# LSTM cross-attention step: first exponential's sum on VectorE, first alpha copy on ScalarE, and three reorderings

## What is computed

```python
def attend(h):
    q = h @ Wq.T
    scores = jnp.einsum('bc,bsc->bs', q, context)
    alpha = jax.nn.softmax(scores, axis=-1)
    ctx = jnp.einsum('bs,bsc->bc', alpha, context)
    return jnp.tanh(jnp.concatenate([ctx, h], axis=-1) @ Wout.T + b_out)

def step(carry, x_t):
    h, c, attn = carry
    inp = jnp.concatenate([x_t, attn], axis=-1)
    gates = inp @ W_ih.T + b_ih + h @ W_hh.T + b_hh
    i, f, g, o = jnp.split(gates, 4, axis=-1)
    c = jax.nn.sigmoid(f) * c + jax.nn.sigmoid(i) * jnp.tanh(g)
    h = jax.nn.sigmoid(o) * jnp.tanh(c)
    out = attn_out = attend(h)
    return ((h, c, attn_out), out)
```

## Time and profile before

| | us |
|---|---|
| median of 3 runs (lowest, highest) | 5821.21 (5819.37, 5823.24) |
| the profiled execution, its own time | 5820.65 |
| its span, first to last instruction | 5818.9 |
| busy: TensorE products | 5284.4 (91%) |
| busy: VectorE | 3434.9 (59%) |
| busy: ScalarE | 1981.9 (34%) |
| busy: GpSimd | 347.5 (6%) |

### The profile page before, as it was taken

One profiled execution on the slowest core, in us unless ns is written; L12 is line 12 of the kernel. 1 busy time (PEld: TensorE's weight loads), 2 busy tenths in 40 slices (PEclk: granted clock), 3 DMA queues, 4 the chain that ended last, 5 costly groups with the idle time before them and its releaser, 6 DMA issues. The chain is left out here.

```text
span 5818.9 us, 383675 instructions
## 1 busy us (share of the span) xinstructions
PE 5284.4 (91%) x171240; PEld 3831.9 (66%) x171240; DVE 3434.9 (59%) x15922; ACT 1981.9 (34%) x7977; POOL 347.5 (6%) x795
## 2 busy tenths in 40 slices
PE   9899999999999999999999999998788879797989
PEld 4677777777777777777777777776534334443433
DVE  5455555555555555555555555554698999999931
ACT  2233343434333343434343434333222222223221
POOL 0000000000000000000000000000111111112100
PEclk9999999999999999999999999999888889898989
DMA  2000000000000000000000000002211101010111
GB/s 98 35 2 2 2 2 2 2 2 2 2 2 2 2 2 2 2 2 2 2 2 2 2 2 2 2 2 59 70 44 42 41 18 54 27 51 29 53 37 54
DMA packets 45677, 111.60 MB, mean 19 GB/s; under 512 B 8192, under 2 KB 10240, under 8 KB 45072
## 3 DMA queue, kind: packets, MB, share of 16 engines
q1 hardware_dynamic: 44144, 109.39, 6.0%
q10 hardware_dynamic: 1440, 1.06, 0.1%
HBM read 99.90 MB, written 10.52 MB: 19 GB/s over the span
## 5 line engine op out<-in xcount | busy, mean ns | idle before, releaser
L850 PE MATMUL lstm_part_ps<-lstm_keys,lstm_hid 128*4 128x128 f32 x32768 | 1023.8, 273 | 205.8 <-DVE lstm_hid L1019 205.8
L850 PEld LDWEIGHTS lstm_part_ps<-lstm_keys,lstm_hid 128*4 128x4 f32 x32768 | 770.0, 86 | 428.9 <-DVE lstm_hid L1019 415.2
L866 PE MATMUL lstm_ctx_ps<-lstm_values,lstm_alpha 128*4 128x128 f32 (+1 forms) x49152 | 1050.9, 237 | 0.0
L866 PEld LDWEIGHTS lstm_ctx_ps<-lstm_values,lstm_alpha 128*4 128x4 f32 x49152 | 903.1, 86 | 91.1
L1048 DVE TENSOR_REDUCE lstm_neg_max<-lstm_part_ps 128x1 f32<-128x128 f32 x1024 | 299.0, 292 | 677.7 <-PE lstm_part_ps L850 677.7
L982 ACT ACTIVATE lstm_expo<-lstm_part_ps,lstm_neg_max 128x128 f32<-128x128 f32 x1024 | 377.1, 368 | 861.1 <-DVE lstm_neg_max L1048 861.1
L1001 DVE STREAM_TRANSPOSE lstm_gates<-lstm_half_ps 128x96 f32<-128x96 f32 x1026 | 290.0, 283 | 599.7 <-PE lstm_half_ps L809 575.7
L809 PE MATMUL lstm_half_ps<-lstm_w_hid,lstm_hid 128*13 128x96 f32 x16384 | 601.2, 245 | 1.4 <-issue 1.4
L809 PE MATMUL lstm_half_ps<-lstm_w_attn,lstm_attn 128*13 128x96 f32 x16448 | 448.2, 246 | 1.4 <-issue 1.4
L809 PEld LDWEIGHTS lstm_half_ps<-lstm_w_hid,lstm_hid 128*13 128x13 f32 x16384 | 379.9, 93 | 1.5 <-issue 1.5
L2082 ACT ACTIVATE mix_gated<-mix_gate_ps 115x512 f32<-115x512 f32 (+2 forms) x200 | 112.6, 563 | 778.6 <-PE mix_gate_ps L1810 778.5
(11 more groups left out here) (324 smaller groups left out, 8341.8 us busy)
## 6 DMA issues: line engine op xcount, KB each, us to landing
mix_ring<-in_sm_chunks SPq DMA_DIRECT2D x120, 358.0 KB, 2.9
mix_ring<-in_mix_chunks SPq DMA_DIRECT2D x80, 384.0 KB, 3.0
lstm_xg<-xg_rows SPq DMA_DIRECT2D x514, 16.0 KB
xg_rows<-rec_lam SPq DMA_DIRECT2D x16, 512.0 KB, 2.6
xT<-in_xT SPq DMA_DIRECT2D x4, 512.0 KB, 8.1
ctxT<-in_ctxT SPq DMA_DIRECT2D x1, 2048.0 KB, 14.3
out_xT<-xT SPq DMA_DIRECT2D x4, 512.0 KB, 3.8
lstm_w_x<-in_lstm_w_x SPq DMA_DIRECT2D x1, 1024.0 KB, 16.9
```

What stands on the lines that cost most here:

```text
L850: mm = pe.matmul(part_rows(score_ps[part], b), hid[:, k, lo:lo + SPACE], keys[:, k, b * SRC + c * P:b * SRC + (c + 1) * P], start=(n == 0 ...
L866: mm = pe.matmul(part_rows(ctx_ps[n], b), alpha[:, b, c, SPACE - 1 - c:2 * SPACE - 1 - c], values[:, b * SC + c, ctx_cols[n]], start=(c == ...
```

## The change

It touches the step loop of the LSTM stage, on three engines.

- ScalarE: the first exponential of a step has no `accum_out`. Behind it ScalarE waits for `turn(0)` and copies the turned exponentials of part 0 into `alpha`, raising a semaphore of that part's own; then it takes the second exponential, with `accum_out` as before.
- VectorE: it no longer copies part 0's alphas. Behind the common maximum it takes the sum of part 0's exponentials by a reduction over 128 columns, copies part 1's alphas, and only then puts the sums side by side. The row's own factor is picked ahead of the weighing of the sums, and the selection matrix is scaled by it ahead of the reciprocal.
- TensorE: `half_hid(0, 1)` runs ahead of `select(0)` and its waits; `half_hid(1, 1)` stays behind it. The waits for alpha are on the two parts' own semaphores.

```diff
--- before.py
+++ after.py
@@ -748,6 +748,7 @@
             max_spread = q.sem("lstm_max_spread")
             max_all_ready = q.sem("lstm_max_all_ready")
             shrink_ready = q.sem("lstm_shrink_ready")
+            first_total_ready = q.sem("lstm_first_total_ready")
             total_spread = q.sem("lstm_total_spread")
             total_ready = q.sem("lstm_total_ready")
             own_ready = q.sem("lstm_own_ready")
@@ -755,7 +756,7 @@
             sel_shrunk_ready = q.sem("lstm_sel_shrunk_ready")
             sel_ready = q.sem("lstm_sel_ready")
             alpha_turned = q.sem("lstm_alpha_turned")
-            alpha_ready = q.sem("lstm_alpha_ready")
+            alpha_ready = [q.sem(f"lstm_alpha{part}_ready") for part in range(PARTS)]
             ctx_ready = [q.sem(f"lstm_ctx{n}_ready") for n in range(PIECES)]
             out_row_ready = [q.sem(f"lstm_out_row{o}_ready") for o in range(KC)]
             attn_summed = [q.sem(f"lstm_attn{o}_summed") for o in range(KC)]
@@ -780,6 +781,12 @@
 
             def by_part(ap):
                 return ap.rearrange("p (a c) -> p a c", a=PARTS)
+
+            def alpha_rows(part):
+                return alpha[:, :, 2 * part:2 * part + 2, SPACE - 1]
+
+            def turned_rows(part):
+                return turned_ps[part].rearrange("p (b r) -> p b r", r=2)
 
             @block.sync
             def _(sp):
@@ -926,22 +933,22 @@
                         turn(0)
                         hidden_part()
                         half_hid(0, 0)
-                        pe.wait_ge(alpha_ready, 2 * t + 1)
+                        pe.wait_ge(alpha_ready[0], t + 1)
                         for n in range(PIECES):
                             context(0, n)
                         pe.wait_ge(exp_ready, 2 * t + 2)
                         turn(1)
                         for n in range(PIECES):
                             context(1, n)
-                        pe.wait_ge(alpha_ready, 2 * t + 2)
+                        pe.wait_ge(alpha_ready[1], t + 1)
                         for n in range(PIECES):
                             context(2, n)
                             context(3, n).then_inc(ctx_ready[n], 1)
                         half_hid(1, 0)
+                        half_hid(0, 1)
                         pe.wait_ge(sel_ready, t + 1)
                         pe.wait_ge(out_row_ready[0], t + 1)
                         select(0)
-                        half_hid(0, 1)
                         half_hid(1, 1)
                         pe.wait_ge(out_row_ready[1], 2 * t + 2)
                         select(1)
@@ -980,7 +987,10 @@
                         for part in range(PARTS):
                             act.wait_ge(max_ready, 2 * t + part + 1)
                             act.activation(expo[:, part, :], score_ps[part], ACT.Exp, bias=neg_max[:, part:part + 1],
-                                           accum_out=total[:, part:part + 1]).then_inc(exp_ready, 1)
+                                           accum_out=total[:, 1:PARTS] if part == 1 else None).then_inc(exp_ready, 1)
+                            if part == 0:
+                                act.wait_ge(alpha_turned, 2 * t + 1)
+                                act.copy(alpha_rows(0), turned_rows(0)).then_inc(alpha_ready[0], 1)
                         act.wait_ge(max_all_ready, t + 1)
                         act.activation(by_part(shrink[:, :]), spread_values(spread_max[:, :]), ACT.Exp, scale=-1.0,
                                        bias=neg_max_all[:, :]).then_inc(shrink_ready, 1)
@@ -1018,11 +1028,6 @@
                     dve.wait_ge(o_turned, t + 1)
                     dve.scalar_tensor_tensor(out=by_batch(hid[:, k, PAD:]), in0=by_batch(o_col[:, k, :]), scalar=1.0,
                                              in1=tanh_c[:, k, :], op0=ALU.add, op1=ALU.mult).then_inc(h_ready[k], 1)
-
-                def keep_turned(t, part):
-                    dve.wait_ge(alpha_turned, 2 * t + part + 1)
-                    turned = turned_ps[part].rearrange("p (b r) -> p b r", r=2)
-                    dve.tensor_copy(alpha[:, :, 2 * part:2 * part + 2, SPACE - 1], turned).then_inc(alpha_ready, 1)
 
                 for ps in (*half_ps, *part_ps, *ctx_bank):
                     dve.memset(ps[:, :], 0.0)
@@ -1047,26 +1052,29 @@
                             dve.wait_ge(scores_ready, 2 * t + part + 1)
                             dve.tensor_reduce(neg_max[:, part:part + 1], score_ps[part], AX_X, ALU.max, negate=True)\
                                .then_inc(max_ready, 1)
-                        keep_turned(t, 0)
                         dve.wait_ge(max_ready, 2 * t + 2)
                         dve.transpose(spread_blocks(spread_max[:, :]), every_row(neg_max[:, :])).then_inc(max_spread, 1)
                         dve.wait_ge(max_spread, t + 1)
                         dve.tensor_reduce(neg_max_all[:, :], spread_values(spread_max[:, :]), AX_XY, ALU.min)\
                            .then_inc(max_all_ready, 1)
+                        dve.wait_ge(exp_ready, 2 * t + 1)
+                        dve.tensor_reduce(total[:, 0:1], expo[:, 0, :], AX_X, ALU.add).then_inc(first_total_ready, 1)
+                        dve.wait_ge(alpha_turned, 2 * t + 2)
+                        dve.tensor_copy(alpha_rows(1), turned_rows(1)).then_inc(alpha_ready[1], 1)
+                        dve.wait_ge(first_total_ready, t + 1)
                         dve.wait_ge(exp_ready, 2 * t + 2)
                         dve.transpose(spread_blocks(spread_total[:, :]), every_row(total[:, :])).then_inc(total_spread, 1)
-                        keep_turned(t, 1)
                         dve.wait_ge(shrink_ready, t + 1)
+                        dve.scalar_tensor_tensor(out=own_terms[:, :], in0=shrink[:, :], scalar=1.0, in1=own_part,
+                                                 op0=ALU.mult, op1=ALU.mult, accum_out=own_shrink[:, :]).then_inc(own_ready, 1)
                         dve.wait_ge(total_spread, t + 1)
                         dve.scalar_tensor_tensor(out=by_part(weighed[:, :]), in0=by_part(shrink[:, :]), scalar=1.0,
                                                  in1=spread_values(spread_total[:, :]), op0=ALU.mult, op1=ALU.mult,
                                                  accum_out=total_sum[:, :]).then_inc(total_ready, 1)
-                        dve.scalar_tensor_tensor(out=own_terms[:, :], in0=shrink[:, :], scalar=1.0, in1=own_part,
-                                                 op0=ALU.mult, op1=ALU.mult, accum_out=own_shrink[:, :]).then_inc(own_ready, 1)
+                        dve.wait_ge(own_ready, t + 1)
+                        dve.tensor_scalar(sel_shrunk[:, :], sel_batch, own_shrink[:, 0:1], None, ALU.mult).then_inc(sel_shrunk_ready, 1)
                         dve.wait_ge(total_ready, t + 1)
                         dve.reciprocal(inverse[:, :], total_sum[:, :]).then_inc(inverse_ready, 1)
-                        dve.wait_ge(own_ready, t + 1)
-                        dve.tensor_scalar(sel_shrunk[:, :], sel_batch, own_shrink[:, 0:1], None, ALU.mult).then_inc(sel_shrunk_ready, 1)
                         dve.wait_ge(inverse_ready, t + 1)
                         dve.wait_ge(sel_shrunk_ready, t + 1)
                         dve.scalar_tensor_tensor(out=sel_scaled[:, :], in0=sel_shrunk[:, :], scalar=inverse[:, 0:1],
```

## The result

| | before | after |
|---|---|---|
| median, us | 5821.24 | 5745.18 |
| lowest and highest of 4 runs | 5819.37, 5823.24 | 5744.19, 5745.92 |
| profiled span | 5818.9 | 5742.4 |

A forecast was written before the change was run, and what follows sets the result against it. The prediction took each LSTM step to be bound by a dependency ring from h through softmax, contexts, selection and gates back to h. It saved 0.085 us by 512 steps, 43.5 us, nothing else: 5778 us, range 5750 to 5804.

The forecast's parts named there:

- the 0.05 belongs to the pair of waits, goes with it, and I take 0: TensorE's 0.05 us idle ahead of select(0) was put down to its two waits; moving half_hid(0, 1) would gain 0.
- Rival A: The gap ahead of the first selection goes too: 0.135 us a step, 69 us, total 5752; chance 12%.
- young waits: Argument for the gap ahead of select(0) vanishing: the price of the two waits might lie in their being young.
- the row's lateness: Alternative reading of the gap ahead of select(0): the output row arrives late; the total would then be 26 us less.
- the accumulator read: ScalarE's read for the first exponential's sum; without it, release at 7.74 instead of 7.83 and turn(0) 0.09 us earlier.
- the 0.085: Forecast gain ahead of the first contexts on TensorE: start at 8.34 in place of 8.42, 0.085 us a step.
- two causes in one wait: Ahead of the first context, the accumulator read and VectorE's maximum of part 1 before the alpha copy both cause the wait.
- the second exponential is not late: On ScalarE behind the new copy, it starts at 8.25 or at worst 8.29; nothing to 0.02 us is lost.
- VectorE's sum is hidden: The new sum of part 0 takes 0.29 us and ends before the second alpha copy, with 0.14 to spare.
- the tail's reordering: VectorE's new order up to the selection matrix: ready about 10.25, needed at 10.54, slack 0.2 or more, no gain or loss.
- Rivals B to E: B: half gain, 5800, 13%; C: ScalarE's queue, 5849, 5%; D: VectorE bound, 5854, 2%; E: edit without effect, 5821, 6%.

The follow-up runs named there:

- a_sum_on_act: Changed kernel with the first exponential's sum back on ScalarE and VectorE's sum dropped, first alpha copy still on ScalarE: 5789.54 us.
- b_sum_on_dve: Kernel before with only the first sum moved to VectorE, both alpha copies staying on VectorE: 5780.72 us.
- a_old_pe_order: Changed kernel with half_hid(0, 1) put back behind the first selection: 5775.14 us.
- b_sum_and_swap: Kernel before with the first sum on VectorE and the two waits ahead of select(0) in the other order: 5747.83 us.
- a_old_order_swapped: Changed kernel with half_hid(0, 1) behind select(0) again and the two waits ahead of select(0) in the other order: 5742.81 us.
- a_copy_on_dve: Changed kernel with the first alpha copy back on VectorE, the first sum still on VectorE: 5746.76 us.
- a_sum_twice: Changed kernel with VectorE's sum of part 0 taken twice, the extra one into a spare column nobody reads: 5749.31 us.
- a_sum_thrice: Changed kernel with VectorE's sum of part 0 taken three times, the extra ones into a spare column nobody reads: 5912.19 us.

## Why the prediction was wrong

*The step that failed* is "the 0.05 belongs to the pair of waits, goes with it, and I take 0". The observation was right (a gap where there are two waits, none where there is one), and so were the numbers of rows 6. The inference wasn't: I set the copy's end at 10.37, added the 0.05 of a single wait, and held the row to be there by 10.42, before TensorE was free at 10.46. I had no measure for a release through a pair. It stood in the same rows, had I measured from the release and not from the products ahead: 10.37 to 10.51 is 0.14, and in rows 8 the semaphore raised at 12.17 and the product at 12.31 are 0.14 again. That semaphore is raised by the first of two transposes of 283 ns, and as at the selection it is the second written of its pair:

```profile
2011.88 0.61 DVE L1001 STREAM_TRANSPOSE lstm_gates<-lstm_half_ps 128x96 f32<-128x96 f32 x2 [1.11 <-PE lstm_half_ps L809]
```

Two places with one and the same distance from their release are two late releases. A cost of the pair itself would have shown the same distance from the products ahead, and there they differ, 0.05 and 0.13. What the runs showed in place of my 0: the output row's release, written second, reaches the first selection late, and that costs 0.06 a step. Moving the products gives 30 us in the kernel before, taking the move out of the changed kernel loses 30, and swapping the two waits gives 29 with no product moved. The Trainium skill ("Perfetto Trace Analysis", Identifying Dependency Chains) says that separate semaphore instructions may stand ahead of an instruction with several waits. No row here shows them, and that nothing would be gained was my conclusion, not the page's. Rival A had the size (5752 for 5745) with the chance of 12%, but not the cause: it spoke of young waits. The true cause stood in the prediction only as a price, the row's lateness, 26 us.

*Right:* the accumulator read. `turn(0)` at 0.42 as said, 512 reads in place of 1024, the copy of 0.17, the contexts at 0.96 for 0.97. It is 0.09 a step for the 0.085, and 44 us of the result by a_sum_on_act. The small excess is the copy's start: 0.31 behind `turn(0)`, where I took 0.33 from `select(1)` and its tanh.

*Right for a wrong reason:* the same 0.085 was put down to two causes in one wait. The sum alone brings 39 us and the copy's move alone nothing that can be told. In the earlier trace rows the copy's start at 8.20 beside the maximum's end at 8.21 is a coincidence: it is 0.32 behind `turn(0)`, which is what a copy behind a turn takes. I had that number and used it for the forecast, but not as a check of the story.

*Right:* the second exponential is not late (0.87), VectorE's sum is hidden (0.28 us for the 0.29, and 0.3 of slack rather than 0.14), the tail's reordering counts for nothing. Rivals B to E did not happen.

*Open:* a rest of some us. Put into the kernel before, the sum's move gives 39 us and the products' move 30, which leaves 7 of the 76; taken out of the changed kernel they cost 44 and 30, which leaves 2. The sum's move is worth 5 us more in the changed kernel, and the copy's move can account for that: once the sum is gone from ScalarE, a copy on VectorE lets the contexts start at 0.97 and one on ScalarE at 0.96, and 0.01 a step is 5 us. The pairs that differ by the copy and by VectorE's order say the same, 5780.7 against 5775.1 (b_sum_on_dve, a_old_pe_order) and 5747.8 against 5742.8 (b_sum_and_swap, a_old_order_swapped); a_copy_on_dve by itself lost only 1.6. So 2 to 5 us is the most that these runs tell of it. The second copy's new place, ahead of the transpose of the sums, was not tried by itself.

## What to carry to other kernels

Where a TensorE product has two waits, try writing the one that ends last first, or putting work ahead of the pair: in this kernel the exchange of two lines was worth half a per cent (29 us of 5821). Only this one pair was tried. To read a gap, measure it from both ends, from the work ahead and from the release, and compare with a second place of the same kind; the distance that stays the same points to the cause, and one swapped line tests it. And a sum that comes as a second instruction holds the semaphore of the first: where its readers don't need the sum, take it elsewhere, so long as that engine has the slack.

## What the runs showed that was not expected

VectorE starts a copy 0.08 us before the end of the reduction ahead of it, as its rows give that end (2002.37 and 2002.45, and again in a_sum_twice and a_sum_thrice), so its queue blocks a ready instruction for less than the rows suggest. TensorE's first product behind a pair of waits starts 0.14 us after the release where the last release is the second written; where it is the first written, the weight load starts about 0.05 after it. And an accumulator read on ScalarE, a row of 0.19 us, delays its release by 0.09 only, since it starts before its exponential ends.
